# Moments by an accumulating add and a squares pass, and a bias added on the vector engine, in the expert stage of a graph network kernel

## The reference, cut to what matters

```python
edge_index = jnp.stack([src, dst])
x = x + gnn(_layernorm(x, axis=-1), edge_index, ...)        # three layers
x = x + moe(_layernorm(x, axis=-1)[None], ...)[0]           # the expert stage

def _layernorm(x, axis=-1, eps=1e-05):
    m = jnp.mean(x, axis=axis, keepdims=True)
    v = jnp.var(x, axis=axis, keepdims=True)
    return (x - m) / jnp.sqrt(v + eps)

def moe(xf):                                                # D=512, F=64, E=8, K=2
    probs = jax.nn.softmax(xf @ Wr + br, axis=-1)
    vals, idx = jax.lax.top_k(probs, K)
    cw = (one_hot(idx, E) * vals[..., None]).sum(axis=1)
    for W1e, b1e, W2e, b2e, cwe in experts:
        h = jax.nn.relu(xf @ W1e + b1e)
        acc = acc + cwe[:, None] * (h @ W2e + b2e)
```

## Time and profile before

| | |
|---|---|
| time, median of 3 runs | 2564.85 us (2563.92 to 2568.93) |
| the profiled execution's own time | 2563.35 us, span 2561.7 us |
| PE busy over the span | 2512.7 us (98%) |
| DVE busy | 1899.7 us (74%) |
| ACT busy | 1485.4 us (58%) |
| POOL busy | 1043.6 us (41%) |
| expert stage, first router product to the last result | 1926.6 to 2559.3 us |
| one tile of it in the steady part | 7.91 us |

### The profile page before, as it was taken

One profiled execution on the slowest core, in us unless ns is written; L12 is line 12 of the kernel. 1 busy time (PEld: TensorE's weight loads), 2 busy tenths in 40 slices (PEclk: granted clock), 3 DMA queues, 4 the chain that ended last, 5 costly groups with the idle time before them and its releaser, 6 DMA issues.

```text
span 2561.7 us, 40284 instructions
## 1 busy us (share of the span) xinstructions
PE 2512.7 (98%) x9906; PEld 1632.2 (64%) x9906; DVE 1899.7 (74%) x5059; ACT 1485.4 (58%) x3471; POOL 1043.6 (41%) x1293
## 2 busy tenths in 40 slices
PE   8999999999999999999999999999999999999999
PEld 4444445555488875555468885555547888888887
DVE  5555555556599976555589996557748999999997
ACT  2222245555288865555458885555525666666665
POOL 3222245555244435555333333555533333333332
PEclk9999999999999999999999999999999999999999
DMA  4444468888355548888735556998842334533331
GB/s 148 132 133 133 129 190 262 271 265 272 100 165 165 164 159 272 267 271 264 229 105 165 163 167 230 320 323 259 268 147 89 100 100 141 168 100 96 100 102 63
DMA packets 208171, 460.91 MB, mean 180 GB/s; under 512 B 34895, under 2 KB 35207, under 8 KB 208004
## 3 DMA queue, kind: packets, MB, share of 16 engines
q0 software_dynamic: 64928, 207.55, 28.6%
q1 hardware_dynamic: 73812, 125.17, 14.1%
q10 hardware_dynamic: 69264, 126.12, 13.4%
HBM read 245.32 MB, written 213.93 MB: 179 GB/s over the span
## 4 chain that ended last, share of the span: by engine, by line
PE 93%; DVE 3%; issue 1%; DMA 1%; ACT 1%; ACTq 0%; another core or an unknown queue 0%; POOL 0%; DVEq 0%; SPq 0%; POOLq 0%
PE psY L678 11%; PE psY L792 9%; PE psM L792 9%; PE psH L792 8%; PE psY L692 6%; PE psY L700 6%; PE psY L709 6%; PE psT L658 5%; PE psS L804 4%; PE psS L805 4%; PE psY L879 3%; PE psH L913 3%; PE psH L926 3%; PE psY L882 3%; PE psY L891 3%; PE psH L917 3%
## 5 line engine op out<-in xcount | busy, mean ns | idle before, releaser
L564 POOL DMA_INDIRECT rows<-y_rows,lists x471 | 491.3, 1043 | 471.9 <-PE psS L805 318.4
L1336 DVE TENSOR_TENSOR lows<-rows,highs 128x512 fp32r<-128x512 f32 x471 | 325.9, 692 | 356.0 <-ACT highs L960 322.2
L960 ACT ACTIVATE outs<-psS 128x512 f32<-128x512 f32 x471 | 279.5, 593 | 282.5 <-PE psS L805 249.2
L960 ACT ACTIVATE highs<-rows 128x512 fp32r<-128x512 f32 x471 | 294.7, 626 | 147.4 <-ACT outs L960 95.7
L804 PE MATMUL psS<-highs,sel 128*128 128x512 f32 x471 | 346.5, 736 | 13.0 <-ACT outs L960 8.4
L571 POOL DMA_INDIRECT rows<-sum_rows,nodeI x158 | 210.3, 1331 | 312.9 <-DVE rows L1344 297.2
L678 PE MATMUL psY<-wy,res 128*128 128x512 f32 x632 | 286.5, 596 | 0.0
L960 ACT ACTIVATE outs<-psY 128x512 f32<-128x512 f32 x237 | 141.6, 598 | 231.2 <-PE psY L678 221.5
L792 PE MATMUL psM<-wz,res 128*128 128x512 f32 x544 | 255.4, 592 | 0.0
L792 PE MATMUL psY<-wz,res 128*128 128x512 f32 x536 | 251.7, 592 | 0.0
L792 PE MATMUL psH<-wz,res 128*128 128x512 f32 x528 | 247.9, 592 | 0.0
(11 more groups left out here) (204 smaller groups left out, 4918.3 us busy)
## 6 DMA issues: line engine op xcount, KB each, us to landing
sum_rows<-outs ACTq DMA_DIRECT2D x471, 256.0 KB
y_rows<-outs SPq DMA_DIRECT2D x237, 256.0 KB, 2.0
rows<-in_x POOLq DMA_DIRECT2D x78, 256.0 KB, 3.2
outs<-in_x SPq DMA_DIRECT2D x78, 256.0 KB
out_rows<-res SPq DMA_DIRECT2D x78, 256.0 KB, 2.0
rows<-y_rows,lists POOLq DMA_INDIRECT x471
z_rows<-res SPq DMA_DIRECT2D x13, 512.0 KB
res<-z_rows SPq DMA_DIRECT2D x13, 512.0 KB, 4.0
```

The lines of the kernel that those rows point to most:

```text
L564: pool.indirect_dma_start(out=rows[:, t % RING, :], out_offset=None, in_=y_d, in_offset=bass.IndirectOffsetOnAxis(ap=col(srcT, t), axis=0) ...
L960: act.activation(o, i_, ACT.Copy).then_inc(signal, 1)
L1336: dve.tensor_tensor(lows[:, t % RING, :], rows[:, t % RING, :], highs[:, g, :].bitcast(F32), ALU.subtract)\
```

## The change

Three edits in the expert stage:

1. **Moments.** bn_stats, bn_aggr and the add of EPS on DVE go, and two carrying memsets with them. The add L1517 becomes a `scalar_tensor_tensor` that also writes the row sum (`XSUM`) and raises `var_in`. POOL makes the negative mean from it (`negative_mean`), ACT squares the centred tile and writes the sum of squares (`squares`, a new pass over 128x512), and POOL makes variance, power and shift (`scale_shift`, now three instructions).
2. **b1.** DVE scales the first product and adds b1 in the same instruction (`up_wide`, now on DVE, behind the smallest logit). ACT's `up_wide` goes, and PE's product L893 with it.
3. **Set-up.** The tiles `twos` and `b1s` are no longer made; b1 is loaded broadcast over the partitions.

```diff
@@ sync: make_room
-                load_row(b1raw, b1.rearrange("e f -> (e f)"), ex_in)
+                load_row(b1row, b1.rearrange("e f -> (e f)"), ex_in)
@@ gpsimd
+            def negative_mean(k):
+                s, n = k % 2, k // 2
+                pool.wait_ge(var_in[s], uses(s) + n + 1)
+                pool.tensor_scalar(st[:, s, MEAN:MEAN + 1], st[:, s, XSUM:XSUM + 1], -1.0 / D, None, ALU.mult)\
+                    .then_inc(mean_in, 1)
+
             def scale_shift(k):
                 s, n = k % 2, k // 2
-                rstd(n, s, 1)
+                pool.wait_ge(square_in, k + 1)
+                pool.tensor_scalar(st[:, s, VAR:VAR + 1], st[:, s, XSQ:XSQ + 1], 1.0 / D, EPS, ALU.mult, ALU.add)\
+                    .then_inc(variance_in, 1)
+                pool.wait_ge(variance_in, k + 1)
+                pool.tensor_tensor(st[:, s, RSTD:RSTD + 1], st[:, s, VAR:VAR + 1], half, ALU.pow)\
+                    .then_inc(rstd_in[s], 1)
                 pool.wait_ge(rstd_in[s], uses(s) + n + 1)
-                pool.tensor_scalar(st[:, s, SHIFT:SHIFT + 1], st[:, s, MEAN:MEAN + 1], st[:, s, RSTD:RSTD + 1], -1.0,
-                                   ALU.mult, ALU.mult).then_inc(shift_in[s], 1)
+                pool.tensor_tensor(st[:, s, SHIFT:SHIFT + 1], st[:, s, MEAN:MEAN + 1], st[:, s, RSTD:RSTD + 1], ALU.mult)\
+                    .then_inc(shift_in[s], 1)
...
             gather_own(1, xn_ready, LAYERS)
+            negative_mean(0)
+            negative_mean(1)
             scale_shift(0)
...
             for k in range(NT):
                 gates(k)
                 if k + 2 < NT:
-                    scale_shift(k + 2)
+                    negative_mean(k + 2)
                 if k + 4 < NT:
                     gather_own(k + 4, var_in, 1)
+                if k + 2 < NT:
+                    scale_shift(k + 2)
@@ tensor: up_across
-                                   start=False, stop=False, skip_group_check=True)
-                pe.matmul(psY[s][:, :], twos[:, :], b1s[:, :], start=False, stop=True, skip_group_check=True)\
-                  .then_inc(y_ps[s], 1)
+                                   start=False, stop=(q == C - 1), skip_group_check=True)
+                mm.then_inc(y_ps[s], 1)
@@ scalar
-            def up_wide(k):
-                s, n = k % 2, k // 2
-                act.wait_ge(ll_ps, (LAYERS - 1) * NT + k + 1)
-                act.activation(psY[s][:, :], psY[s][:, :], ACT.Copy, scale=1.0 + 1.0 / STEP).then_inc(wide[s], 1)
+            def squares(k):
+                s, n = k % 2, k // 2
+                act.wait_ge(mean_in, k + 1)
+                act.activation(rows[:, 2 + s, :], kept(place(k)), ACT.Square, bias=st[:, s, MEAN:MEAN + 1],
+                               accum_out=st[:, s, XSQ:XSQ + 1]).then_inc(square_in, 1)
...
+            squares(0)
+            squares(1)
             norm(0)
             x_top(0)
             for k in range(NT):
...
                 exps(k)
-                up_wide(k)
                 if k + 1 < NT:
                     x_top(k + 1)
                 if k >= 2:
                     widen_down(k - 2)
+                if k + 2 < NT:
+                    squares(k + 2)
@@ vector: split_small
-                link(dve.tensor_tensor(two_rows, ident[:, 0:1], ident[:, 1:2], ALU.add))
-                dve.tensor_scalar(twos[:, :], iota[:, :], 0.0, two_rows, ALU.is_ge, ALU.mult).then_inc(ex_set, 1)
-                link(copy(b1high.bitcast(F32R), b1raw))
-                link(dve.tensor_tensor(b1raw, b1raw, b1high, ALU.subtract))
-                link(dve.tensor_scalar(b1raw, b1raw, ident[:, 1:2], None, ALU.mult))
-                link(dve.scalar_tensor_tensor(b1s[:, :], b1high, ident[:, 0:1], b1raw, ALU.mult, ALU.add))
-                dve.sem_inc(ex_set, 1)
@@ vector
+            def up_wide(k):
+                s, n = k % 2, k // 2
+                dve.wait_ge(ll_ps, (LAYERS - 1) * NT + k + 1)
+                dve.scalar_tensor_tensor(psY[s][:, :], psY[s][:, :], 1.0 + 1.0 / STEP, b1row, ALU.mult, ALU.add)\
+                   .then_inc(wide[s], 1)
@@ vector: experts
                     dve.tensor_reduce(stat(LOWEST), gate(LG), AX.X, ALU.min).then_inc(lg_sb[s], 1)
+                    up_wide(k)
...
-                    k_x = step(dve.tensor_tensor(own_x, q, v, ALU.add))
+                    dve.scalar_tensor_tensor(own_x, q, 1.0, v, ALU.mult, ALU.add, accum_out=stat(XSUM))\
+                       .then_inc(var_in[s], 1)
...
-                if ahead:
-                    after(k_x)
-                    carry(2)
-                    k_bn = step(dve.bn_stats(stat(STAT, 6), own_x))
                 if own:
                     after(k_idx)
                     dve.tensor_copy(stat(IDX, 2), smi[:, 0:2]).then_inc(top_set, 1)
-                if ahead:
-                    after(k_bn)
-                    carry(3)
-                    k_var = step(dve.bn_aggr(stat(MEAN, 2), stat(STAT, 6)))
-                if ahead:
-                    after(k_var)
-                    variance(s)
```

More of the change, by code:

```diff
@@ L113, in build @@
         LG, EX, TOP, CW, HIGH, LOW = (X * k for k in (0, 1, 2, 3, 4, 6))
+        XSUM, XSQ = 0, 1
         STAT, MEAN, VAR, RSTD, SHIFT, LOWEST, SUM, INV, IDX, TOPW = 0, 6, 7, 8, 9, 10, 11, 12, 13, 15
@@ L135, in build @@
         wg2 = nc.alloc_sbuf_tensor_at("wg2", [P, C, 2 * X], F32R, offset=res_at + 48 * D)
[L136 to L139, removed]
+        b1row = res[:, 13, :]
         down_raw = nc.alloc_sbuf_tensor_at("down_raw", [P, C, D], F32, offset=res_at + 56 * D)
@@ L289, in build @@
         pad_set = sem("pad_set")
+        mean_in = sem("mean_in")
+        square_in = sem("square_in")
+        variance_in = sem("variance_in")
         block = ctx.enter_context(nc.Block())
@@ L934, in _ @@
             all_turns(pe, z_sb, LAYERS)
-            pe.wait_ge(ex_set, 2 * C + 3)
+            pe.wait_ge(ex_set, 2 * C + 1)
             for k in range(NT):
```

## The result

The changed kernel takes 2620.92 us (2618.30 to 2622.39, 4 runs) against 2564.39 before: ratio 1.022, interval [1.0206, 1.0235]. It is slower by 56.5 us. The forecast was 2629, with a range of 2604 to 2654. The profiled execution has a span of 2616.6 us, 54.9 more than before.

A forecast was written before the change was run, and what follows sets the result against it. PE and DVE were both taken as full before; a new one-tile loop of 8.79 us against 7.91 would then bound. 2563.35 + 67.8 (77 x 0.88) - 1.4 - 2.2 = 2627.5, 1.5 more for the median: 2629, range 2604 to 2654.

The forecast's parts named there:

- The loop: Expert stage, one tile: cast's end, gates, negative mean, squares, h_high, h_low, rest of DVE's pass; 8.79 us against 7.91.
- T0: End of DVE's cast L1529, which raises the signal for POOL's gates; at 2207.50 in the tile before the change.
- POOL's place for the gates: First step on POOL, from the end of DVE's cast L1529 to the next instruction behind the gates: 1.24 us.
- The rest of DVE's pass: DVE from h_low to the end of cast L1529: 5.71, cast 0.49 earlier, scaling 0.60, row sum 0.10: 5.92 us.
- the row sum: Accumulated sum in DVE's add: its price put between 0 and 0.20 us a tile, 0.10 taken.
- The gains at the start: Expert stage's set-up and start: two PE waits go, 1.4 and 2.2 us less.
- the two places: PE's 1.41 us wait while twos and b1s are made, and its 2.22 us wait for an add; both would go.
- DVE's wait: DVE would stand about 1.0 us ahead of h_low in every tile, released by ACT's h_high.
- rival 1: Other loops bound, through POOL's late shift and the exponentials or, over two tiles, PE's transposes: 8.5 us, 2607; chance 0.07.
- Rival 2: ACT's idle time hides the squares; DVE sets the pace at 7.78 us a tile, 2551; chance 0.04.
- Rival 3: DVE's add with row sum is dear, some 0.5 us more: 9.3 a tile, 2668; chance 0.05.
- Rival 4: PE's clock dips through idle time, a microsecond or two each; above 2650 only if many tiles dip; chance 0.03.

The follow-up runs named there:

- the ordered moments: Kernel before with only the moments part, POOL's negative mean ahead of the gates and gather behind the shift; b1 product on PE, scaling on ACT: 2559.59 us.
- POOL's order is changed: Changed kernel with POOL's negative mean ahead of the gates and its gather behind variance, power and shift: 2542.76 us, ratio 0.9918 to the kernel before.

## Why the prediction was right

**What bounded the kernel before** was read rightly: both PE and DVE. The b1 part alone shows DVE at its end (0.54 a tile for one more pass), the ordered moments show PE at its own (7.89, with DVE 479 of 540 busy).

**The loop and its steps.** The time from T0 to h_low was given as 2.87 and is 2.87, with each step within 0.03: POOL's place for the gates 1.26 (1.24 given), negative mean 0.24 (0.26), squares and their read 0.72 together (0.71), h_high 0.58 (0.60). The rest of DVE's pass was given as 5.92 and is 2205.49 - 2199.72 = 5.77. That is the term that was mis-sized: the row sum, for which I took 0.10, costs nothing (2204.32 to 2204.91 is the same 0.59 as the plain add's place), and the scaling starts 0.07 behind the smallest logit where its predecessor came 0.12 behind it. Hence 8.64 a tile and not 8.79; over 77 tiles that is 12 us, more than the whole distance from 2629 to 2621.

**The gains at the start** were right at the two places (both waits are gone, 4.0 us together against the 3.6 given), but I counted the filling tiles at the steady price, and they gave back about 4: the first h_low is no earlier than before. PE is busy 1.15 of 3 us from 1926 to 1929, and from 1931 to 1935 its granted clock is 0.50 (1.2 GHz) with every microsecond busy. DVE's scaling now waits for these products:

```profile
1934.74 0.70 DVE L1489 SCALAR_TENSOR_TENSOR psY<-psY,res 128x512 f32<-128x512 f32 x1 [2.52 <-PE psY L898]
```

Before, too, a stretch at 0.50 stood there, but the scaling was not on DVE. Summed over stretches of 1 us from 1926 to 1940, the clock was at 0.50 for about 3.4 us before and about 6.8 us after, which takes at most 1.7 us more of PE's time (an estimate: half of the difference). So the clock alone does not account for the 4 us. PE's first hidden transposes start at 1937.00, and started at 1939.34: 2.3 us earlier, so 1.7 of the 4.0 are lost up to there. The other 2.4 are lost behind them, and that is the new loop itself. Before, h_high followed these transposes; now it stands behind the squares of a later tile, and h_low at 1940.76 comes exactly 2.87 behind that pass's T0 (1937.89):

```profile
1939.43 0.72 ACT L1090 ACTIVATE rows<-res,st 128x512 f32<-128x512 f32 x1 [3.06 <-POOL st L621]
```

No run parts these shares, and fillings differ: the kernel with the doubled squares, which has more to do, reached its first h_low at 1938.48.

This miss and the one above have opposite signs and cancel in part. That the forecast is 8 us off, and not 12, is luck.

**DVE's wait.** I expected about 1.0 ahead of h_low. It is 0.53 there and 0.33 ahead of the last add; counted against a place of 0.60 each, the two delays are 0.62 and 0.41, so the sum is right. A wait ahead of the last add was my own sign for rival 1, so the profile by itself did not decide between the two. The runs do: with the gather last, that wait is gone, all of it is at h_low with 0.95, and the tile stays at 8.64; with the squares doubled the tile grows by the whole pass. So the loop is right, and the place of part of the wait was not foreseen. PE's wait ahead of the transposes is 0.75 where about 1 was given, and its busy share 91% where 87% was.

**Rival 1** did exist just beneath: 8.34 in the version with the squares behind h_high, where 8.45 to 8.55 was given. **Rival 2** needed T0 to h_low within 1.9; it holds once POOL's order is changed, and then the kernel is faster, though by PE's 7.66 rather than DVE's 7.78. **Rival 3**, the rule of the Trainium skill in "Vector Engine (DVE) Microarchitecture Reference", section "Points that are easy to get wrong", does not hold for this form: with two fp32 inputs from SBUF and a row sum the instruction takes 0.67, the plain one 0.68. **Rival 4**: the clock stayed at 1.00 with 490 of 540 us busy.

## What to carry to other kernels

Work moved to idle engines is free only where nothing in a loop waits for it: follow the new signal around, engine by engine in program order, until it comes back to its start, and compare that length with the tile's period. A value that is ready early (the row sum, 0.5 us ahead of T0) should be consumed ahead of what is ready late, on an engine that executes in order; and long issues such as a gather go behind what others wait for. Where two engines are full, as here, a shift of work from one to the other pays only after the receiver has been given room, so such parts have to be judged together.

## What the runs showed of the hardware

- A `scalar_tensor_tensor` with a row sum on DVE costs no more than a plain add of the same size: a read of 0.08 us that starts with the next instruction.
- A squares pass with one pointer operand takes 0.72 us for 128x512 and its read 0.19, of which ACT's queue sees 0.72 in all.
- On POOL the gap ahead of a gather is 0.36 behind the negative mean, which need not wait, and 0.53 to 0.54 where the gather stands directly behind the gates or behind the new shift (0.43 behind the old one): taking the negative mean out ahead of it gained 0.04, not 0.24.
